# Two attention layers on one core: layer 1's output bank, half of its residual, and the places of maxima, sums and value products

## The reference, cut to what matters

```
layer 0:  q = Wq x + bq, k = Wk x + bk (32 rows each), v = Wv x + bv (256 rows)
          attn = softmax over i of q[:, i] . k[:, j]      (4096 x 4096)
          x1 = gamma0 * (v attn) + x
layer 1:  theta = conv(x1), phi = maxpool2(conv(x1)), g = maxpool2(conv(x1))   (1024 keys, 128 rows of g)
          attention = softmax over the 1024 keys of theta . phi
          y = gamma1 * (out_w (g attention) + out_b) + x1
```

## Time and profile before

| | us |
|---|---|
| median of 3 runs | 2683.14 (2678.57 to 2683.64) |
| profiled execution, its own time | 2681.38 |
| its span | 2679.4 |
| PE busy | 2597.6 |
| DVE busy | 2015.5 |
| POOL busy | 1981.5 |
| ACT busy | 1746.0 |

### The profile page before, as it was taken

One profiled execution on the slowest core, in us unless ns is written; L12 is line 12 of the kernel. 1 busy time (PEld: TensorE's weight loads), 2 busy tenths in 40 slices (PEclk: granted clock), 3 DMA queues, 4 the chain that ended last, 5 costly groups with the idle time before them and its releaser, 6 DMA issues. The chain is left out here.

```text
span 2679.4 us, 38539 instructions
## 1 busy us (share of the span) xinstructions
PE 2597.6 (97%) x11696; PEld 2077.7 (78%) x11696; DVE 2015.5 (75%) x3352; ACT 1746.0 (65%) x3182; POOL 1981.5 (74%) x1560
## 2 busy tenths in 40 slices
PE   7999999999999999999999999999999999999988
PEld 6788888877778888887777888887777788888756
DVE  6688888777768887876776787887687678877665
ACT  6666666675776666666587666666558766666566
POOL 5677777665897777775699777776569877777668
PEclk9999999999999999999999999999999999999989
DMA  2000000110120000011022000001002100000012
GB/s 91 1 16 17 25 16 20 37 48 17 59 82 26 17 24 17 17 40 40 17 72 79 24 17 16 17 17 47 24 17 88 63 17 16 17 17 16 22 43 71
DMA packets 47656, 88.97 MB, mean 33 GB/s; under 512 B 5344, under 2 KB 5472, under 8 KB 47456
## 3 DMA queue, kind: packets, MB, share of 16 engines
q1 hardware_dynamic: 46896, 85.73, 9.7%
q10 hardware_dynamic: 560, 0.79, 0.1%
HBM read 52.70 MB, written 33.55 MB: 32 GB/s over the span
## 5 line engine op out<-in xcount | busy, mean ns | idle before, releaser
L635 POOL TENSOR_TENSOR prob_l<-prob,prob_h 128x512 fp32r<-128x512 f32 x1280 | 1647.3, 1300 | 650.9 <-PE o_ps L1049 569.7
L694 ACT ACTIVATE prob<-s_ps 128x512 f32<-128x512 f32 x1280 | 767.1, 599 | 771.8 <-PE s_ps L1020 755.2
L879 DVE TENSOR_REDUCE mx<-aux 128x1 f32<-128x512 f32 x1161 | 794.9, 686 | 306.8 <-PE aux L1082 301.7
L1045 PE MATMUL o_ps<-prob_h,vh 128*128 128x512 f32 x2304 | 912.5, 396 | 7.9 <-ACT osb L708 4.9
L1048 PE MATMUL o_ps<-prob_l,vh 128*128 128x512 f32 x2304 | 907.0, 394 | 9.0 <-POOL prob_l L635 7.8
L1049 PE MATMUL o_ps<-prob_h,vl 128*128 128x512 f32 x2304 | 901.4, 391 | 0.0
L841 DVE TENSOR_TENSOR acc<-prob,acc 128x512 f32<-128x512 f32 x1187 | 814.9, 687 | 76.1 <-ACT prob L694 56.5
L697 ACT ACTIVATE prob_h<-s_ps 128x512 fp32r<-128x512 f32 x1280 | 764.9, 598 | 0.0
L1020 PE MATMUL s_ps<-queries,keys 128*128 128x512 f32 x1280 | 523.4, 410 | 23.8 <-DMA queries<-nm_turned 22.7
L1048 PEld LDWEIGHTS o_ps<-prob_l,vh 128*128 128x128 f32 x2304 | 434.5, 189 | 117.7 <-POOL prob_l L635 26.1
L1045 PEld LDWEIGHTS o_ps<-prob_h,vh 128*128 128x128 f32 x2304 | 434.9, 189 | 114.9 <-ACT osb L708 22.2
(11 more groups left out here) (126 smaller groups left out, 1787.2 us busy)
## 6 DMA issues: line engine op xcount, KB each, us to landing
xa<-x SPq DMA_DIRECT2D x32, 512.0 KB, 3.6
xp<-x SPq DMA_DIRECT2D x32, 512.0 KB, 3.6
spill<-xa SPq DMA_DIRECT2D x32, 512.0 KB, 2.8
xa<-spill SPq DMA_DIRECT2D x32, 512.0 KB, 3.6
y<-xa SPq DMA_DIRECT2D x32, 512.0 KB, 2.8
queries<-nm_turned SPq DMA_DIRECT2D x256, 1.0 KB
xp<-spill SPq DMA_DIRECT2D x3, 512.0 KB, 4.6
prob<-w_in ACTq DMA_DIRECT2D x1, 640.0 KB, 5.6
```

Of the source, the lines that this page charges most:

```text
L635: nc.gpsimd.tensor_tensor(out=prob_l[:, i, :], in0=prob[:, i, :], in1=prob_h[:, h % RING, :].bitcast(f32), op=ALU.subtract).then_inc(pl_re ...
L694: nc.scalar.activation(prob[:, h % PRING, :], s_ps[s][:, :], ACT.Exp).then_inc(p_ready, 1)
L879: ins = nc.vector.tensor_reduce(out=dst, in_=bank[:, :], axis=AX.X, op=ALU.max)
L1045: mm(o_ps[ct][:, :], value(vh, l, t, ct), prob_h[:, i, :], start=t == 0, stop=False)
```

## The change

- **Output bank.** In layer 1 the output of chunk n goes to `o_ps[n % 2]` instead of always `o_ps[0]`, and the waits of the first value products change with it.
- **Maxima.** The maxima for chunk n+2 of layer 1 move from bank `Y` to `X2`, and from place 3 of steps 4 to 7 to place 3 of steps 1, 3, 5 and 7. Two further maxima of the last image, n = 4 and 5, move from `X1` to `X2`. Before the last image's layer 1 one maximum moves from `Y` to `O0`.
- **Residual.** For the half k = 1, ScalarE's copy and GpSimd's addition are replaced by one scalar_tensor_tensor of VectorE, which multiplies the product in PSUM by gamma1 and adds `xa`. The bias `cb` of this half is added to `xa` before, by a new ScalarE job XC; in most chunks that is done in layer 0, behind the rounding of x1, and the store to `spill` waits for it. The product Z of k = 1 moves one step forward, to bank `X1`.
- **N** in front of layer 1: the second half moves from step 2 to step 6.
- **Narrow D1** of (0,b,6) and (0,b,7), b < 3, moves from step 31, place 2, to step 0, place 1, of the next chunk.
- **Last chunk (0,b,7):** K0(0) and K0(1) and their low parts move to later places, five value entries from (3,0) to (4,1) too, and some maxima.

```
+def output_bank(l, n):
+    return l * n % 2
...
-KEYS0 = ((0, (1, 1), X1, (2, 1)), (1, (3, 1), X1, (4, 1)), (2, (12, 1), X1, (13, 1)), (3, (14, 1), X1, (15, 1)),
+KEYS0 = ((0, (2, 1), X1, (3, 1)), (1, (3, 3), X1, (4, 3)), (2, (12, 1), X1, (13, 1)), (3, (14, 1), X1, (15, 1)),
...
-           (3, 0, (16, 3), X2, (17, 3)), (3, 1, (18, 1), X2, (19, 1)), (4, 0, (19, 3), X2, (20, 3)),
-           (4, 1, (21, 1), X2, (22, 1)), (5, 0, (24, 3), X2, (25, 3)), (5, 1, (26, 1), X2, (27, 1)),
+           (3, 0, (17, 1), X2, (18, 1)), (3, 1, (18, 3), X2, (19, 3)), (4, 0, (20, 3), X2, (21, 1)),
+           (4, 1, (21, 3), X2, (22, 3)), (5, 0, (24, 3), X2, (25, 3)), (5, 1, (26, 1), X2, (27, 1)),
...
-MAXIMA1 = ((0, 3, X0), (1, 3, X0), (2, 3, X0), (3, 1, X0), (3, 3, X0), (4, 3, X0), (5, 3, X0), (6, 3, X0))
+MAXIMA1 = ((0, 3, X0), (1, 3, X0), (2, 3, X0), (3, 3, X0), (4, 1, X0), (5, 1, X0), (5, 3, X0), (6, 3, X0))
...
+        if own_x1(b, c):
+            put(g + xl[1][0] + 1, 1, Job("XC", 1, b, c, 0))
...
+        if (more or not last_of_image) and not first_of_later:
             put(g + KT[0], 1, on(Job("D1", 0, b, n, 0), X1))
         else:
             put(g + KT[0] - 1, 2, on(Job("D1", 0, b, n, 0), X1))
...
-    st = [maxima(1, b, 0, 1, s, (X1, Y, S1, X2)[s]) for s in range(SUBS)]
+    st = [maxima(1, b, 0, 1, s, (X1, O0, S1, X2)[s]) for s in range(SUBS)]
...
-    before[GATE] = [d2, *add, *rnd, k1, k1k, g1, k1m, t1, *st, Job("M", 1, b, 0, 0), k1q, k1l, t1l]
+    before[GATE] = [d2, *add, *rnd, k1, k1k, g1, k1m, t1, *st, Job("M", 1, b, 0, 0), Job("XC", 1, b, c, 0), k1q, k1l, t1l]
...
+            if n == 0 and not own_x1(b, 0):
+                put(g + 4, 1, Job("XC", 1, b, 0, 0))
...
-                    put(g + 2 + 2 * k, 3, on(Job("Z", *prev, k), X0))
-                    put(g + 2 + 1 + 2 * k, 3, Job("ZA", *prev, k))
+                    put(g + 2 + k, 3, on(Job("Z", *prev, k), (X0, X1)[k]))
+                    put(g + 3 + 2 * k, 3, Job("ZA", *prev, k))
...
-                        put(g + 5 + i, 1, maxima(1, b, NCH - 1, 0, 2 * (n - 4) + i, X1))
+                        put(g + 5 + i, 1, maxima(1, b, NCH - 1, 0, 2 * (n - 4) + i, X2))
...
-                    put(g + 1 + k, 1, Job("N", *first, k))
+                    put(g + 1 + 5 * k, 1, Job("N", *first, k))
...
-                for s, (t, place) in enumerate(((4, 3), (5, 3), (6, 3), (7, 3))):
-                    put(g + t, place, maxima(1, b, n + 2, 1, s, Y))
+                for s, t in enumerate((1, 3, 5, 7)):
+                    put(g + t, 3, maxima(1, b, n + 2, 1, s, X2))
...
                 if l:
-                    sp.wait_ge(y_ready, CT * image0(b, n) + CT)
+                    sp.wait_ge(y_ready, image0(b, n) + 1)
+                    wait_free(sp, Job("Z", 1, b, n, 1))
+                elif own_x1(b, n):
+                    sp.wait_ge(bias_ready, BIAS_NO[Job("XC", 1, b, n, 0)] + 1)
...
+                elif name == "XC":
+                    if own_x1(b, c):
+                        slot, _ = a_slot(0, b, c)
+                        act.wait_ge(xl_ready, CT * ROUND[Job("X", 1, b, c, 0)] + CT)
+                    else:
+                        slot, turn = a_slot(1, b, c)
+                        act.wait_ge(xa_in[slot], 16 * (turn + 1))
+                    nc.scalar.activation(xa[slot][:, 1, :], xa[slot][:, 1, :], ACT.Identity,
+                                         bias=cb[:, 1:2]).then_inc(bias_ready, 1)
...
+                elif name == "ZA" and k == 1:
...
+                    nc.vector.scalar_tensor_tensor(
+                        out=xa[slot][:, 1, :], in0=aux[BANK[product]][:, :], scalar=cols[:, COL_G1:COL_G1 + 1],
+                        in1=xa[slot][:, 1, :], op0=ALU.mult, op1=ALU.add).then_inc(free[BANK[product]], 1)
...
+                elif t == 0 and chunk_before(l, b, n) is not None and chunk_before(l, b, n)[0] == 1:
+                    pe.wait_ge(o_act, chunk_no(l, b, n))
...
+                out = o_ps[ct if l == 0 else output_bank(l, n)]
```

More of the change, by code:

```diff
@@ L387 @@
         ROW_OF[_job] = len(ROW_OF)
+    if _job.name == "XC":
+        BIAS_NO[_job] = len(BIAS_NO)
     if _job.name == "K0":
@@ L550, in read @@
                 sp.wait_ge(xl_ready, CT * ROUND[job._replace(name="X", k=0)] + CT)
-                if l == 1 and own_x1(b, c):
-                    reload(0, b, c)
                 if (l, b, c) in X_USE:
@@ L581, in entry @@
                 name, l, b, c, k = job
-                if name in ("N", "ZA") and k == CT - 1:
+                if name == "ZA" and k == CT - 1 or name == "N" and k == CT - 1 and not own_x1(b, c):
                     store_a(l, b, c)
+                elif name == "XC" and own_x1(b, c):
+                    store_a(0, b, c)
                 elif name == "XL" and k == CT - 1:
@@ L601, in _ @@
                 for g in range(TILES):
-                    for job in late.get(g, ()):
-                        reload(*job[1:4])
+                    for chunk0 in late.get(g, ()):
+                        reload(*chunk0)
                     l, b, n, t = tile_at(g)
@@ L608, in _ @@
                         entry(job)
+                        if job.name == "XC":
+                            late.setdefault(g + 2, []).append((0, *job[2:4]))
                     for e in DURING.get(g, ()):
@@ L611, in _ @@
                         _, l, b, c, k = e.job
-                        if e.job.name in ("N", "ZA") and k == CT - 1 and (l == 1 or not own_x1(b, c)):
-                            late.setdefault(g + 2, []).append(e.job)
+                        if e.job.name == "ZA" and k == CT - 1 or e.job.name == "N" and k == CT - 1 and not own_x1(b, c):
+                            late.setdefault(g + 2, []).append((l, b, c))
+                        elif e.job.name == "XC" and own_x1(b, c):
+                            late.setdefault(g + 2, []).append((0, b, c))
                 for job in END:
@@ L717, in copy_acc @@
                     seconds = SECOND_BEFORE[l, b, n]
-                    wait(act, y_ready, CT * (seconds - 1) + 1 if prev[0] else CT * seconds)
+                    wait(act, y_ready, seconds)
                 nc.scalar.activation(psums[:, :] if wide(l, b, n) else zc[:, 0, :], acc[:, :],
@@ L1030, in attend @@
                         prev = chunk_before(l, b, n)
[L1031 to L1036 removed]
+                        if prev is None:
+                            wait_free(pe, LAST_ON_Y[b])
+                        elif l == 0 or n == 0:
+                            pe.wait_ge(o_act, chunk_no(l, b, n) - prev[0])
+                        elif n > 1:
+                            pe.wait_ge(o_act, chunk_no(l, b, n) - 1)
+                        if l == 0 and prev is not None and prev[0] == 0:
+                            pe.wait_ge(o_dve, image0(*prev[1:]) + 1)
+                        if l == 1 and n == 1:
+                            pe.wait_ge(o_dve, image0(*((b + 1, 0) if b + 1 < B else (b, NCH - 1))) + 1)
                         if (h, O0) in LAST_ON:
@@ L1071, in entry @@
                 wait(pe, free[at], USE[job])
-                if at == Y and (l or b):
-                    pe.wait_ge(o_dve, image0(*((b + 1, 0) if b + 1 < B else (b, NCH - 1))) + 1)
+                if at == O0 and b > 0:
+                    pe.wait_ge(o_act, chunk_no(0, b, NCH - 1) + 1)
                 if name == "ST":
```

29 lines of the change are left out of this document (15 added, 14 removed).

## The result

| | before | after |
|---|---|---|
| median of the runs | 2682.4 (4 runs, 2678.57 to 2683.64) | 2652.38 (4 runs, 2651.61 to 2654.53) |
| profiled execution | 2681.38 | 2652.04 |
| its span | 2679.4 | 2650.2 |

The ratio is 0.9891, with a 95% interval of 0.9879 to 0.9903: 30 us faster. The forecast was 2651, with a range of 2642 to 2667. The total is right to 1.4 us. Its parts are not, and that they cancel is luck: the last chunks of layer 0 gave a third less than forecast, layer 1 and the last image more.

A forecast was written before the change was run, and what follows sets the result against it. TensorE was taken to bound the kernel at 97% busy, with GpSimd bounding layer 1 from n=4. Gains of 25.95 (three images), 4.5 (narrow sums) and 1.85 (last image), 32.3 us together, gave 2651; range 2642 to 2667.

The forecast's parts named there:

- GpSimd bounds layer 1, and half the residual relieves it: Layer 1 from n=4 on: ten GpSimd instructions of 1.245 us become nine, 11.2 us a chunk; gain 3.4 us per image.
- Rival C: Layer 1 does not follow GpSimd; ScalarE is the second bound near 12.3, layer 1 gives 3 us: 2662; chance 0.08.
- Rival B: GpSimd and VectorE shut each other out at layer 1's new instruction; n=6 and 7 0.75 us longer each: 2657; chance 0.12.
- This I take as TensorE's floor: Layer 1, chunk n=2: its 12.13 us with TensorE busy all through was taken as the least TensorE needs.
- This edit ... has no term of its own: Alternating output banks and maxima on X2 in layer 1: they only keep the 11.2 us, own gain 0.
- N's second half, 1.2 an image: Layer 1, n=0: moving it five steps after the first removes part of 1.7 us TensorE idle; 1.2 taken, bounds 0 and 1.7.
- Narrow sums, 4.5: (0,b,6) and (0,b,7): the sums' matmuls fill the 0.75 us wait for ScalarE's copy, 6 chunks, 4.5 us.
- Keys and values, 4.05 an image: (0,b,7): moved keys net 0.3 us loss, moved values gain 0.45 and 2.2, slow clock 1.7; bounds 0 and 5.5.
- 1.7 an image for the slow clock: (0,b,7): the granted clock of 0.50 right behind V0(4,0)'s wait goes when that wait goes, 1.7 us.
- Last image, 1.85: Layer 1 of the last image: small chunk gains, less 1.5 us each at n=4 and 5, tail 1.4; sum 1.85 us.
- A: Layer 1 gains, the last chunk of layer 0 does not, since VectorE blocks its stalls: 2664; chance 0.15.
- D: Slower: layer 1's row of maxima becomes the bound; at 2.5 us late 42 us are lost: 2693; chance 0.04.

The follow-up runs named there:

- last experiment: The combined kernel (changed kernel with other places for last-image maxima, K0 and first maxima of (0,b,7)) with both residual halves on VectorE: 2638.02 us, ratio 0.9832.
- one-bank kernel: Changed kernel, but layer 1's output stays on one bank and each chunk's first value product waits for ScalarE's copy: 2661.64 us in one run.
- first attempt at better places: Changed kernel with last-image maxima on X0, and K0(1), the last chunk's first maxima, V0(4,0) and V0(4,1) moved: 2653.61 us, ratio 0.9899.

## Why the prediction was right in the whole, and where its steps failed

**GpSimd bounds layer 1, and half the residual relieves it: right.** 9 x 1.245 = 11.2 was forecast for n = 6 and 7, and they take 11.24 and 11.22. With the half put back, 12.24 and 12.41. One sign did not come: GpSimd was to have idle time in n = 6 and 7, and has 0.43 in n = 6 and none in n = 7. It is still the bound of n = 7, which falls to 10.89 when the other half goes too. Rival C (ScalarE near 12.3) is refuted by the same rows.

**Rival B: did not come, but was no test of the rule behind it.** The new VectorE instruction takes 0.75, and GpSimd works off nine pieces beside it in 11.22, not 11.95. B came from a rule of the Trainium skill (SBUF — State Buffer, section "SBUF: two separate sides") on VectorE instructions with two SBUF inputs. The new instruction has one tile in SBUF; the other is in PSUM, and what else it reads from SBUF is a column of scalars, which by these rows does not act as a second input. So B priced it by a rule that does not reach it. The kernel does have an instruction with two tiles in SBUF, the first sum in most chunks of layer 0 (`acc` = `prob` + `prob`, L866), and there the trace of the changed kernel agrees with the rule:

```profile
1259.59 1.29 POOL L655 TENSOR_TENSOR prob_l<-prob,prob_h 128x512 fp32r<-128x512 f32 x1 [0.70 <-PE o_ps L1095]
1259.72 1.72 DVE L866 TENSOR_TENSOR acc<-prob 128x512 f32<-128x512 f32 x1
```

Started 0.13 behind a split, the sum takes 1.72 and ends 0.56 after it. The same sum of the kernel before, at 1271.61, had no split beside it and took 0.68. Where the sum starts first (440.94, 0.70 long), the split that starts 0.18 behind it takes 1.65 and not 1.28.

**"This I take as TensorE's floor": failed.** Layer 1 gave 16.3 us and not 13.8. The 12.13 of the earlier trace rows was made of work, 0.23 us at two maxima whose bank came free just when they were due, and 0.14 of slightly wider distances. With the maxima two steps apart 11.74 remain, and they remain when GpSimd has a piece less still (last experiment). The step from "busy 12.13 of 12.13" to "floor" was the error. The 12.13 of the one-bank kernel is a coincidence: there it is 0.39 of waiting for the copy.

**"This edit ... has no term of its own": failed.** Alternating banks is worth 0.39 in every chunk, 9.3 us in the total of one run; maxima apart 0.92 in each of n = 3 to 5. The residual alone, which I gave the whole of the 3.4 an image, gives nothing. Three bounds lie close to GpSimd's 12.45: the maxima's bank with the residual in VectorE's queue (12.6), ScalarE's copy (12.13), and TensorE's work (11.74). Against the 296.3 of before, the three images gain nothing with the residual alone, 0.9 without it, 3.6 without the places of the maxima, 5.0 without the alternation, and 15.4 with all three. Banks alone and places alone were not run. That the sum of layer 1 came out nearly right is luck: the joint gain was laid to one edit.

**N's second half, 1.2 an image: mis-sized, 0.4.** The bounds were 0 and 1.7. I knew that the queue has to work it off and still took more than half; the chunk after pays nearly all back.

**Narrow sums, 4.5: right**, 1.5 an image by the experiment, 4.6.

**Keys and values, 4.05 an image: failed, 2.0 to 2.4, and most of that is the clock.** The first key stall went (1.2) and the second came with 1.47 for 1.5. What was missed is that the maxima moved with the keys come close to one another: 0.40 and 0.72 of new waiting. And V0(4,0) kept 0.61 where 0 was forecast. The net of the key part is a loss of 1.75, not of 0.3. V0(3,0) (0.20 left, 0.18 forecast) came out, and of the 2.2 from V0(4,0) 1.6 came. Of the 1.7 an image for the slow clock, 1.6 is in the two traces in each of three images; but in image 0 it stood behind the wait for a row of maxima, which no edit touched, so a third of that term came by luck, and "right behind the longer one" holds for images 1 and 2 alone. Without the clock, (0,1,7) gained 1.2, of which 0.8 is the sums.

**Last image, 1.85: mis-sized, 4.0.** n = 0 to 3 gained 1.1 for 0.1; (1,3,4) and (1,3,5) came out 1.6 longer together, for 2.3 forecast; n = 6 and 7 gained 1.2 for 2.65, since n = 7 still has two waits for splits, 0.18 and 0.28. The end behind the last copy gained 3.3 for 1.4 (13.0 to 9.7). Only 0.85 of it is the residual, since the last sum ended 2.30 behind the last product before and 1.45 after, GpSimd's half being last, and not VectorE's; the rest is the full clock, which I did not count. No experiment shows that the change brought the full clock: in two others whose end is the same, with the maxima close and with the values back, the end took 11.6 and 10.7, again with a low clock.

**Rivals A and D.** A (2664: nothing from the last chunk) fails, 10.6 came from there; but its reason, that an in-order queue gives a delay again later, is what halved the term, and what undid the first attempt at better places. D fails: in (1,0,3) the rows are issued from 722.20, 2.0 us into the chunk, where it was 3.0 before. The 1.6 us that the prediction put in for the landing has no row behind it. Where TensorE stood waiting for rows, it started 1.1 us after the last issue had ended (604.46 and 605.56 before, 2003.93 and 2005.06 after), so there was more to spare than it took.

So 2.5 us more in layer 1 and 2.15 in the last image stand against 6.0 less in the last chunks, and 1.6 more in the first chunk that belong to no edit. The total is near the forecast because these cancel.

What stays open: why the clock fell behind some stalls and not behind others, and whether the low clock of (1,3,0), whose time varied from 40.1 to 43.4 over these kernels, depends on anything in the kernel.
